# Batch 1 of a gated cross-attention block: x scaled and rounded ahead of its context on ScalarE and VectorE

## What is computed

```python
def quant_dequant_act_1x128(x):            # per token and block of 128 features
    safe = max(amax(abs(xb)), 1e-4)
    q = (xb * (448 / safe)).astype(float8_e4m3fn)
    return q * (safe / 448)
# the weight (here the context) likewise, per block of 128 x 128

xq, wq = quant_dequant_act_1x128(layernorm(x)), quant_dequant_weight_128x128(ctx)
x = x + tanh(g_xattn) * einsum('emk,enk->emn', xq, wq)          # batch by batch

h = layernorm(x)
comb = top-4 of softmax(h @ gate_w.T) over 8 experts, renormalised
moe  = sum_e comb[e] * ((silu(h @ wg[e].T) * (h @ wu[e].T)) @ wd[e].T)
sh   = silu(h @ swg.T) * (h @ swu.T) @ swd.T
x = x + tanh(g_ffn) * (moe + sigmoid(h @ shared_gate_w.T) * sh)
```

## Time and profile before

| | |
|---|---|
| median of 3 runs | 185.72 us (185.38 to 185.96) |
| the profiled execution | 185.49 us, of which 183.5 are its span |
| PE busy | 159.0 us, 87% of the span |
| DVE busy | 131.4 us, 72% |
| ACT busy | 103.1 us, 56% |
| POOL busy | 92.7 us, 51% |
| chain that ended last | PE 68%, DVE 14%, ACT 10%, issue 3%, DMA 2% |

### The profile page before, as it was taken

How to read it: one execution, slowest core, us unless ns; L and a number is a source line. 1 busy time by engine, 2 the same in 40 slices (tenths; PEclk the granted TensorE clock), 3 DMA queues, 4 the chain that set the end, 5 groups by cost and what they waited for, 6 DMA issues and landing times.

```text
span 183.5 us, 2313 instructions
## 1 busy us (share of the span) xinstructions
PE 159.0 (87%) x723; PEld 122.7 (67%) x723; DVE 131.4 (72%) x265; ACT 103.1 (56%) x229; POOL 92.7 (51%) x92
## 2 busy tenths in 40 slices
PE   0022688999889999999997999999999999999992
PEld 0010357877568688777885887887886888888871
DVE  1878984897998999999866962977278455444463
ACT  2499563958546886474746764445654554443430
POOL 3120615653744468556317995556545555553450
PEclk9999999999999999999999999999999999999999
DMA  5999992000019940000000000200299400000003
GB/s 140 289 404 340 321 311 86 5 0 0 0 61 272 255 103 4 2 2 0 4 0 0 2 0 0 92 25 0 66 251 269 105 4 0 2 0 0 4 0 114
DMA packets 8049, 16.19 MB, mean 88 GB/s; under 512 B 1235, under 2 KB 1235, under 8 KB 8037
## 3 DMA queue, kind: packets, MB, share of 16 engines
q1 hardware_dynamic: 8036, 16.04, 28.9%
HBM read 14.95 MB, written 1.09 MB: 87 GB/s over the span
## 4 chain that ended last, share of the span: by engine, by line
PE 68%; DVE 14%; ACT 10%; issue 3%; DMA 2%; POOL 0%; DVEq 0%
PE bank L971 58%; ACT xc L380 2%; DMA x<-xs 2%; DVE act L737 2%; DVE x L660 2%; PE bank L923 2%; ACT xc L409 2%; DVE a_lo L753 1%; PE bank L1010 1%; ACT cw L372 1%; DVE bn L571 1%; ACT silu L457 1%; PE bank L1015 1%; PE bank L1011 1%; DVE amax_x L615 1%
## 5 line engine op out<-in xcount | busy, mean ns | idle before, releaser
L315 POOL TENSOR_TENSOR gu_lo<-w_raw,gu_hi 128x512 fp32r<-128x512 f32 (+1 forms) x34 | 47.5, 1398 | 21.6 <-ACT gu_hi L442 13.4
L322 POOL TENSOR_TENSOR d_lo<-w_raw,d_hi 128x256 fp32r<-128x256 f32 (+1 forms) x34 | 32.6, 960 | 44.1 <-ACT d_hi L448 44.0
L971 PE MATMUL bank<-h_hi,gu_hi 128*128 128x512 f32 x124 | 49.6, 400 | 0.5 <-ACT silu L457 0.4
L971 PE MATMUL bank<-h_hi,gu_lo 128*128 128x512 f32 x124 | 49.2, 397 | 0.0
L971 PE MATMUL bank<-h_lo,gu_hi 128*128 128x512 f32 x124 | 49.1, 396 | 0.0
L457 ACT ACTIVATE silu<-bank 128x512 f32<-128x512 f32 (+1 forms) x34 | 20.2, 594 | 45.8 <-PE bank L971 44.7
L747 DVE TENSOR_TENSOR act<-silu,mixw 128x512 f32<-128x512 f32 x18 | 14.7, 814 | 22.0 <-ACT silu L457 22.0
L753 DVE TENSOR_TENSOR a_lo<-act,a_hi 128x512 fp32r<-128x512 f32 x32 | 28.1, 877 | 0.7 <-ACT a_hi L465 0.7
L971 PEld LDWEIGHTS bank<-h_hi,gu_hi 128*128 128x128 f32 x124 | 23.3, 188 | 6.9 <-issue 1.6
L971 PEld LDWEIGHTS bank<-h_hi,gu_lo 128*128 128x128 f32 x124 | 23.3, 188 | 5.5
L971 PEld LDWEIGHTS bank<-h_lo,gu_hi 128*128 128x128 f32 x124 | 23.4, 189 | 5.2
(11 more groups left out here) (117 smaller groups left out, 194.8 us busy)
## 6 DMA issues: line engine op xcount, KB each, us to landing
w_raw<-w_full SPq DMA_DIRECT2D x16, 384.0 KB, 5.2
mixw<-comb_d SPq DMA_DIRECT2D x10, 256.0 KB, 5.7
x<-xs SPq DMA_DIRECT2D x4, 256.0 KB, 6.4
cw<-ctx_t SPq DMA_DIRECT2D x4, 256.0 KB, 5.8
out_t<-fin SPq DMA_DIRECT2D x4, 256.0 KB, 2.3
mixw<-comb_d SPq DMA_DIRECT2D x4, 224.0 KB, 5.6
mixw<-comb_d SPq DMA_DIRECT2D x4, 192.0 KB, 5.5
mixw<-comb_d SPq DMA_DIRECT2D x4, 160.0 KB, 4.9
```

The lines of the kernel that those rows point to most:

```text
L315: nc.gpsimd.tensor_tensor(gu_lo[:, slot, 0:cols], w_raw[:, c, 0:cols], gu_hi[:, slot, 0:cols].bitcast(F32), ALU.subtract).then_inc(gu_lo_d ...
L322: nc.gpsimd.tensor_tensor(d_lo[0:rows, slot, :], w_raw[0:rows, c, at:at + D], d_hi[0:rows, slot, :].bitcast(F32), ALU.subtract).then_inc(d ...
L971: last = nc.tensor.matmul(out, w[k][a], x_of[k][b], start=(start and k == 0 and i == 0), stop=(stop and k == blocks - 1 and i == 2))
```

## The change

For batch 1 `scale_x` and `mags_x` stand ahead of `scale_ctx` and `mags_ctx` on ACT, and `lift_x` and `round_x` ahead of `lift_ctx` and `round_ctx` on DVE. The other renamings in the diff only give the returned step numbers names of their own. No instruction is added or taken away; PE, POOL and SP keep their lists.

```diff
--- before.py
+++ after.py
@@ -474,10 +474,10 @@
             copy_xqt(0)
             a.wait_ge(small_landed, 16)
             nc.scalar.activation(g_tanh[:], small_in[:, 0:2], ACT.Tanh).then_inc(tanh_done, 1)
+            scale_x(1)
+            mags_x(1)
             scale_ctx(1)
             mags_ctx(1)
-            scale_x(1)
-            mags_x(1)
             residual0(0)
             high_gu(1)
             copy_xqt(1)
@@ -781,17 +781,17 @@
             summed_1 = moments(0, 1)
             copy_scales_ctx(0)
             stats(0, 1, summed_1).then_inc(var_ready, 1)
-            lifted = lift_x(0)
-            round_x(0, lifted)
-            lifted = lift_ctx(0)
+            lifted_x0 = lift_x(0)
+            round_x(0, lifted_x0)
+            lifted_c0 = lift_ctx(0)
             max_x_1 = max_x(1)
-            round_ctx(0, lifted)
+            round_ctx(0, lifted_c0)
             scales_x(1, max_x_1)
             dequant_scales(0)
-            lifted = lift_ctx(1)
-            round_ctx(1, lifted)
-            lifted = lift_x(1)
-            round_x(1, lifted)
+            lifted_x1 = lift_x(1)
+            round_x(1, lifted_x1)
+            lifted_c1 = lift_ctx(1)
+            round_ctx(1, lifted_c1)
             residual1(0)
             residual_sum(0)
             stats_x1(0)
```

## The result

| | before | changed |
|---|---|---|
| median | 185.60 us (185.38 to 185.96, 4 runs) | 188.68 us (187.80 to 190.40, 4 runs) |
| ratio to before | | 1.0188, 95% interval 1.0144 to 1.0232 |
| the profiled execution | 185.49 us, span 183.5 | 188.06 us, span 185.9 |

The kernel is slower by 3.5 us (the ratio times 185.60), where 2.2 were forecast. The median stands inside the range of 186.8 to 189.0, the ratio points just past it (189.1). The four runs lie at 187.8, 188.06, 189.29 and 190.4: they spread over 2.6 us, those of before over 0.6. The profiled execution is one of the two low ones.

A forecast was written before the change was run, and what follows sets the result against it. Between 15 and 24 us the lists of ACT and DVE were taken to set the pace. Span 183.5 + 1.57 + 0.79 - 0.13 = 185.73, with 1.99 outside it 187.72; forecast 187.9, range 186.8 to 189.0.

The forecast's parts named there:

- The new wait on ACT: On ACT behind the tanh: scale_x(1) must wait for mul_x of batch 1, so ACT idles 1.57 us.
- The collision: On DVE, the context's lift of batch 1 is held by POOL's low_gu(0) and ends 0.79 us later.
- the 0.13 saved: On DVE, residual_sum(0) has no POOL work beside it and takes 0.69 us instead of 0.82.
- Rival A: The context's lift on DVE gets through without a collision with POOL: delay 1.44 us, time 187.2; chance 0.14.
- From there on: Everything behind the residual sum of batch 0 keeps its distances and order, and all second-part work starts 2.23 us late.
- Rival C: PE's four waits after 34 us, together 2.5 us, absorb the delay: 185.6; chance 0.08 together with the last rival.
- The seven fillers: PE's filler products behind attend(1) move from 21.18 to about 22.3 us and are not on the path.
- B: PE's clock falls behind: the 24 gate_up_first products of batch 0 go at 0.21 us instead of 0.12, 190.4; chance 0.10.
- The argument against B: Against a low PE clock behind the fillers: the burst itself is as long as before.

The follow-up runs named there:

- e11: Changed kernel with POOL's first subtraction waiting for the rounded context of batch 1, and 9 fillers instead of 7; median 187.37 us, ratio 1.0080.
- e3: Changed kernel with POOL's first subtraction waiting for the rounded context of batch 1 instead of the rounded x; median 188.01 us, ratio 1.0109.
- e9: Kernel before with only DVE's part of the change, ACT's order as before; median 189.83 us, ratio 1.0175.
- e5: Changed kernel unaltered, run again beside the kernel before; median 188.89 us, ratio 1.0178.
- e12: Changed kernel unaltered, a third time, on one chip with the version with 11 fillers; median 188.23 us, ratio 1.0131.
- e8: Kernel before with 6 fillers ahead of the transposes of xq of batch 1 and 12 instead of 7 behind attend(1); median 186.33 us, ratio 1.0023.
- e7: Changed kernel with 6 fillers ahead of the transposes of xq, 4 ahead of attend(1), 16 behind it; median 188.49 us, ratio 1.0136.
- e6: Kernel before without any filler products, both calls taken out; median 188.41 us, ratio 1.0135.
- e4: Kernel before with only ACT's part of the change, DVE's order as before; median 188.80 us, ratio 1.0159.
- e10: Kernel before with 6 fillers ahead of the transposes of xq of batch 1, 1 ahead of attend(1), 8 behind it; median 186.29 us, ratio 1.0009.

## Why the prediction was right in its mechanism and too small in its size

- **The new wait on ACT, 1.57 us:** right. ACT starts L380 0.04 us behind the end of `mul_x` (15.28 + 0.16 to 15.48), and e11, where it is nearly all that is left, measures 1.5 us.
- **The collision, 0.79 us, and the 0.13 saved:** right, in the first trace to 0.01 us, and e3 takes just this away. Rival A fell: in the six traces of the changed order with POOL's wait as it was, the lift took 1.48 us each time. Its price was wrong as well. It said that POOL waits if it comes later; e9 has that case, and there POOL's turn came behind the lift and held the rounding instead, so 1.44 us would not have been all.
- **From there on, a shift of 2.23 us with nothing absorbed:** right; the transposes came 2.23 later and PE's four later waits kept their lengths. Rival C fell.
- **The seven fillers "are not on the path":** this is the step that failed. They are not, but they decide at which level the path goes on. I gave B 0.10 and held it to be another case beside the forecast, at 190.4. The runs show an addition to it in a share of the executions: two of three traces of the changed kernel have it (1.26 and 1.19 us), and two of the four runs of the first comparison are above 189. Its size, 2.5, was too large, since I let all 24 products go at the lower level, while the clock rose among them. So the mean effect is 3.5, 3.3 and 2.4 us in three comparisons instead of 2.2, and the range ended at 189.0 where such a share takes the ratio to 189.1.
- The argument against B, that the burst was as long as before, was the weak one, since the rise does not keep to a place in the burst. Before, it came at the seventh filler (3.07 us where seven at the lower level take 3.19); in the first trace of the changed kernel it came behind the seventh, in those of e5 and e12 only among the 24 products. In e8 PE worked from 20.46 on without a gap, and eleven fillers behind `attend(1)` still went at the lower level.
- The port: the Trainium skill (SBUF — State Buffer, "Who interferes with whom") says that whoever starts first has the port for its whole instruction, and e9 agrees for both sides in turn, 1.65 us for POOL and 1.64 for DVE.

**What stays open.** What makes one execution of the same program rise in time and another not isn't seen in a trace; up to the transposes the traced executions of one order differ mainly in when the first transfers land (`mul_x` at 15.12 to 16.01 us over all), and a late landing does not decide it alone (e7 and e3 landed late and had the upper level, e9 and e12 landed late and had not). The share is known roughly only: 2 in 3 by the traces, 5 in 15 by times above 189. e6 and e4 spread more than I can assign. For executions without a trace only the granted clock averaged over the span is on record. It is 0.989 to 0.991 in nine of them, among these the 189.29 of the first comparison, the two highest of e9 and the three highest of e10, but also 186.12 in e8, while the traced executions with the step read 1.00. What it stands for is open. The mark `mul_x` also tends to come later in the traces of the changed order or its halves (seven of ten behind 15.41) than in the five of the old order (15.16 to 15.41). e5 and e12, the same program, differ in it by 0.31, and nothing ahead of it was moved, so I take this for chance, which isn't shown.

## What to carry to other kernels

Ahead of moving a step forward in a list, look when its input is ready: here the work that was moved behind it had been covering just that time, and all 1.57 us of the new wait went to all that stood behind. Then look at what moves on other engines: a DVE instruction with two SBUF inputs that starts while POOL subtracts (or the reverse) waits out the remainder of the other (here 1.48 us instead of 0.69), and a burst of fillers at whose end the clock rises is a part of the schedule, not a spare. When a trace shows the clock rising at the last filler, time several executions: here five of 15 stood above 189 us, where the same order with 11 fillers had none above 188.76.

## What the runs showed of the hardware

- The granted clock read 1.00 in stretches in which 256 columns started 0.22 us apart and in stretches in which they started 0.12 apart. Only the starts told the level.
- The same program went one way and the other: 4.36 us or 5.62 for the same 24 products and what lies around them.
- Between POOL's subtraction and two back-to-back DVE instructions with two SBUF inputs the turn went DVE, POOL, DVE (e9, one trace). The DVE instruction that is held ends 0.55 us behind POOL's, where it takes 0.69 alone (e9; 0.56 in the changed kernel); POOL's, held by the first, ended 1.13 us behind it, where it takes 1.26 alone.
- `attend(1)` and eleven fillers of 512 columns ran at the lower level from 20.46 to 26.0 us without a gap between them, and at 26.25 the upper level was there (e8).
- A pause of 1.26 us left the clock at the upper level once it had risen (e7, one trace).
